# Layer-2 cross-attention: the self-attention's units regrouped across the four row groups of the array

## The reference

```
q, k = rope(x @ Wq), rope(x @ Wk)                    # 128 tokens, 32 heads of 8
w    = softmax(max(q k^T / sqrt(8) + mask, lowest))  # 128 x 128 per head
a_w  = tanh(gate) * softmax(q a_k^T / sqrt(8))       # 128 x 2048 per head: a_k = context @ Wk
out  = (w @ v + a_w @ a_v) @ Wo
```

## Time and profile before

| | |
|---|---|
| three runs | 1271.54, 1272.19, 1277.94 us |
| profiled execution, first to last instruction | 1179.2 us |
| what lies around the span, against the median | 93.0 us |
| PE busy in the span | 1060.2 us (90%) |
| DVE busy | 684.4 us (58%) |
| ACT busy | 486.5 us (41%) |
| main loop of L2X | from 429.8 to 736.5 us of the span |

### The profile page before, as it was taken

The page is one execution under the profiler, slowest core; times in us unless marked ns, Lnnn a source line. Parts: engine busy times, 40 slices in busy tenths (PEclk is TensorE's granted clock), DMA queues, the critical chain, the costliest instruction groups (busy, mean ns, idle before and its releaser), DMA issues.

```text
span 1179.2 us, 23059 instructions
## 1 busy us (share of the span) xinstructions
PE 1060.2 (90%) x9433; PEld 747.2 (63%) x9433; DVE 684.4 (58%) x1528; ACT 486.5 (41%) x1097; POOL 167.7 (14%) x172
## 2 busy tenths in 40 slices
PE   7988899996995999999999999898999990887998
PEld 6866666664884555555555665677566660776776
DVE  4544257775326667765556752454768997555333
ACT  2111137773331335556456568352544540141332
POOL 0002300000000000000000000000777776100000
PEclk9999999997997999999999999899999995988999
DMA  9113300000301200000000000201556554005661
GB/s 357 57 41 121 126 1 2 2 3 29 146 1 51 121 1 1 2 2 2 1 2 2 2 2 2 87 1 62 141 148 187 151 146 123 16 1 223 224 223 54
DMA packets 16727, 84.39 MB, mean 72 GB/s; under 512 B 3184, under 2 KB 4208, under 8 KB 12912
## 3 DMA queue, kind: packets, MB, share of 16 engines
q1 hardware_dynamic: 8432, 57.75, 12.9%
q0 software_dynamic: 8192, 25.17, 7.5%
HBM read 82.65 MB, written 0.26 MB: 70 GB/s over the span
## 4 chain that ended last, share of the span: by engine, by line
PE 71%; DVE 15%; POOL 7%; issue 4%; ACT 2%; DMA 1%; POOLq 0%; SPq 0%; DVEq 0%; ACTq 0%
PE L2X_bank_ring L1799 7%; PE L2X_bank_ring L1815 7%; PE L2X_bank_read L1829 6%; POOL L2F_rows L2532 5%; PE L2X_bank_ring L1738 4%; DVE x L2768 3%; PE L1X_banks_scores L927 3%; PE L2X_bank_ring L1747 3%; PE L3F_bank_y L3409 3%; PE L1A_bank_qk L1192 2%; PE L0X_bank_moments L473 2%; PE L0X_bank_k L462 2%; PE L3F_bank_gate_up L3369 2%; PE L1X_bank_proj L904 2%; PE L1X_bank_read L943 2%
## 5 line engine op out<-in xcount | busy, mean ns | idle before, releaser
L2098 DVE TENSOR_REDUCE L2X_max_parts<-L2X_bank_ring 128x1 f32<-128x512 f32 x256 | 158.3, 683 | 85.9 <-PE L2X_bank_ring L1799 85.9
L2009 ACT ACTIVATE L2X_context_exp<-L2X_bank_ring 128x384 f32<-128x384 f32 (+1 forms) x384 | 144.1, 464 | 63.0 <-PE L2X_bank_ring L1815 60.3
L2532 POOL DMA_INDIRECT L2F_rows<-in_L2F_embed_dram,L2F_expert x128 | 131.7, 1029 | 56.2 <-issue 37.3
L1799 PE MATMUL L2X_bank_ring<-L2X_context_kT,L2X_q_masked 32*128 32x512 f32 x512 | 97.4, 630 | 0.0
L1035 ACT ACTIVATE L1X_probs<-L1X_clipped,L1X_drop,L1X_keep 128x1024 f32<-128x1024 f32 x64 | 77.6, 1237 | 30.7 <-DVE L1X_clipped L1095 23.5
L1095 DVE TENSOR_SCALAR L1X_clipped<-L1X_banks_scores 128x1024 f32<-128x1024 f32 x64 | 75.4, 1220 | 24.6 <-PE L1X_banks_scores L927 22.9
L1815 PE MATMUL L2X_bank_ring<-L2X_q_and_max,L2X_context_kT 32*128 32x384 f32 (+1 forms) x768 | 85.9, 497 | 0.0
L1829 PEld LDWEIGHTS L2X_bank_read<-L2X_context_exp,L2X_context_v_ones 128*32 128x32 f32 x2048 | 50.2, 109 | 43.8 <-issue 33.4
L1829 PE MATMUL L2X_bank_read<-L2X_context_exp,L2X_context_v_ones 128*32 128x128 f32 x2048 | 75.8, 277 | 1.1 <-ACT L2X_context_exp L2009 0.8
L2768 DVE SCALAR_TENSOR_TENSOR x<-L2F_rows,L2F_expert_weight,x 128x256 f32<-128x256 f32 x128 | 62.4, 487 | 4.6
L1799 PEld LDWEIGHTS L2X_bank_ring<-L2X_context_kT,L2X_q_masked 32*128 32x128 f32 x512 | 41.4, 183 | 24.7 <-issue 12.2
(11 more groups left out here) (632 smaller groups left out, 2027.5 us busy)
## 6 DMA issues: line engine op xcount, KB each, us to landing
L3F_expert_weights<-in_L3F_experts_dram SPq DMA_DIRECT2D x16, 1280.0 KB, 5.7
L1A_groups<-in_L1A_groups_dram SPq DMA_DIRECT2D x3, 1536.0 KB, 9.7
L0X_tokens<-in_L0X_tokens_dram SPq DMA_DIRECT2D x8, 512.0 KB, 13.3
ctxT<-in_ctxT_dram SPq DMA_DIRECT2D x7, 512.0 KB, 13.9
slot<-in_L1A_dram SPq DMA_DIRECT2D x1, 3584.0 KB, 11.6
slot<-in_L0F_dram SPq DMA_DIRECT2D x1, 3072.0 KB, 10.9
slot<-in_L2A_dram SPq DMA_DIRECT2D x1, 3072.0 KB, 10.5
slot<-in_L2F_dram SPq DMA_DIRECT2D x1, 2476.5 KB, 9.1
```

Of the source, the lines that this page charges most:

```text
L1799: nc.tensor.matmul(bank[:, :], qm[32 * g:32 * g + 32, b, c, j, :], cT[32 * g:32 * g + 32, s % 3, blk * 512:(blk + 1) * 512], start=True, s ...
L2009: nc.scalar.activation(ex[:, n % NE, g, 0:width(s)], bank_of(s_e, done(n) + g + 1)[:, 0:width(s)], ACT.Exp, scale=SCALE).then_inc(s_e, 1)
L2098: nc.vector.tensor_reduce(parts[:, j, g, blk:blk + 1], bank_of(s_ft, n)[:, :], AX, ALU.max).then_inc(s_ft, 1)
L2532: pool.indirect_dma_start(out=rows[:, r, k, :], out_offset=None, in_=env.dram["L2F_embed"], in_offset=bass.IndirectOffsetOnAxis(idx[:, b, ...
```

## The change: what it does

The 64 heads of the small attention are cut into 16 units instead of 24. A unit is now (s, j): head j of each of the four row groups, so always four heads, and a stage has as many units as a group has heads: three or two. Unit (s, x) takes the places of the old unit of quarter x; quarter 3 of every stage, and quarter 2 too in stages 0 and 5, has none. `self_scores` writes its four products each into a bank of its own in the ring (four places instead of one), and `self_shift` empties them with four instructions of 128 columns; its row maximum, subtraction, the exponential, the four transposes and their copy are 512 columns wide. `self_read` writes to four column groups, `turn_reads` transposes `heads(c)` slices of soT instead of four. The mask is loaded once per batch instead of three times side by side.

```diff
-EXTRA_L2X = {"L2X_mask": lambda i: np.repeat(i["mask_Bx1xSxS_fk0"].reshape(B, 1, P, P), 3, 1).transpose(2, 0, 1, 3).reshape(P, B * 3 * P)}
+EXTRA_L2X = {"L2X_mask": lambda i: i["mask_Bx1xSxS_fk0"].reshape(B, P, P).transpose(1, 0, 2).reshape(P, B * P)}
...
-    maskt = L.sb("mask", [P, B * TRIO])
+    maskt = L.sb("mask", [P, B * P])
...
-    smx = L.sb("self_max", [P, 3])
-    se, spT = L.sb("self_exp", [P, TRIO]), L.sb("self_probsT", [P, TRIO])
-    soT = L.sb("self_readT", [P, NG, P])
+    smx = L.sb("self_max", [P, NG])
+    se, spT = L.sb("self_exp", [P, NG * P]), L.sb("self_probsT", [P, NG * P])
+    soT = L.sb("self_readT", [P, 3, P])
...
-    def heads_read(n):
-
-        return sum(heads(stages[m // NG][1]) for m in range(n))
+    units = [(s, j) for s in range(NSTG) for j in range(heads(stages[s][1]))]
+    NU = len(units)
+
+    def unit(s, x):
+
+        s, x = s + x // 4, x % 4
+        return units.index((s, x)) if (s, x) in units else None
...
         def self_scores(n):
-            (b, c), g = stages[n // NG], n % NG
-            bank = turns.take(pe, s_st, n + 1)
-            for j in range(heads(c)):
-                i = nc.tensor.matmul(bank[:, j * P:(j + 1) * P], qm[32 * g:32 * g + 32, b, c, j, :],
-                                     kT[32 * g:32 * g + 32, c, b, :], start=True, stop=True)
-            i.then_inc(s_ss, 1)
+            (s, j) = units[n]
+            b, c = stages[s]
+            for g in range(NG):
+                bank = turns.take(pe, s_st, NG * n + g + 1)
+                nc.tensor.matmul(bank[:, 0:P], qm[32 * g:32 * g + 32, b, c, j, :],
+                                 kT[32 * g:32 * g + 32, c, b, :], start=True, stop=True).then_inc(s_ss, 1)
 
         def self_turn(n):
             pe.wait_ge(s_se, n + 1)
             bank = turns.take(pe, s_spT, n + 1)
-            for j in range(heads(stages[n // NG][1])):
-                i = nc.tensor.transpose(bank[:, j * P:(j + 1) * P], se[:, j * P:(j + 1) * P], ident)
+            for g in range(NG):
+                i = nc.tensor.transpose(bank[:, g * P:(g + 1) * P], se[:, g * P:(g + 1) * P], ident)
             i.then_inc(s_sturn, 1)
...
         def self_read(n):
-            (b, c), g = stages[n // NG], n % NG
+            (s, j) = units[n]
+            b, c = stages[s]
             pe.wait_ge(s_spT, n + 1)
             bank = turns.take(pe, s_soc, n + 1)
-            for j in range(heads(c)):
+            for g in range(NG):
                 h = head_at(c, g, j)
-                nc.tensor.matmul(bank[32 * j:32 * j + 32, 0:P], svp[:, b, h * VW:h * VW + 32],
-                                 spT[:, j * P:(j + 1) * P], start=True, stop=True).then_inc(s_so, 1)
+                nc.tensor.matmul(bank[32 * g:32 * g + 32, 0:P], svp[:, b, h * VW:h * VW + 32],
+                                 spT[:, g * P:(g + 1) * P], start=True, stop=True).then_inc(s_so, 1)
 
         def turn_reads(s):
-            pe.wait_ge(s_soc, NG * (s + 1))
+            pe.wait_ge(s_soc, units_before(s + 1))
             bank = turns.take(pe, s_sy, s + 1)
-            for g in range(NG):
-                i = nc.tensor.transpose(bank[:, g * P:(g + 1) * P], soT[:, g, :], ident)
+            for j in range(heads(stages[s][1])):
+                i = nc.tensor.transpose(bank[:, j * P:(j + 1) * P], soT[:, j, :], ident)
             i.then_inc(s_sot, 1)
...
-                n, r = NG * s + t // 4, t % 4
+                x, r = t // 4, t % 4
+                n, following, past = unit(s, x), unit(s, x + 1), unit(*(s, x - 1) if x else (s - 1, 3))
                 firsts = first_sets(s, t)
                 second_scores(s, t)
                 if v_tile(s, t):
                     context_v(*v_tile(s, t))
                 if firsts:
                     first_scores(*firsts[0])
-                if r == 3 and n + 1 < NG * NSTG:
-                    self_scores(n + 1)
+                if r == 3 and following is not None:
+                    self_scores(following)
...
-                if r == 0 and n:
-                    self_read(n - 1)
+                if r == 0 and past is not None:
+                    self_read(past)
                 if r == 1 and s + 2 < NSTG:
                     context_k(s + 2, t // 4)
-                if r == 2:
+                if r == 2 and n is not None:
                     self_turn(n)
...
         read(NSTG - 1, NT - 1)
-        self_read(NG * NSTG - 1)
         turn_reads(NSTG - 1)
...
         def self_exp(n):
             act.wait_ge(s_sd, n + 1)
-            wd = width(n // NG)
-            nc.scalar.activation(se[:, 0:wd], se[:, 0:wd], ACT.Exp).then_inc(s_se, 1)
+            nc.scalar.activation(se[:, :], se[:, :], ACT.Exp).then_inc(s_se, 1)
 
         def self_copy(n):
             act.wait_ge(s_sturn, n + 1)
             if n:
-                act.wait_ge(s_so, heads_read(n))
-            wd = width(n // NG)
-            nc.scalar.activation(spT[:, 0:wd], bank_of(s_spT, n + 1)[:, 0:wd], ACT.Copy).then_inc(s_spT, 1)
+                act.wait_ge(s_so, NG * n)
+            nc.scalar.activation(spT[:, :], bank_of(s_spT, n + 1)[:, :], ACT.Copy).then_inc(s_spT, 1)
 
         def self_copy_read(n):
-            s, g = n // NG, n % NG
-            wd = 32 * heads(stages[s][1])
-            act.wait_ge(s_so, heads_read(n + 1))
-            if s and g == 0:
+            s, j = units[n]
+            act.wait_ge(s_so, NG * (n + 1))
+            if s and j == 0:
                 act.wait_ge(s_sot, s)
-            nc.scalar.activation(soT[0:wd, g, :], bank_of(s_soc, n + 1)[0:wd, 0:P], ACT.Copy).then_inc(s_soc, 1)
+            nc.scalar.activation(soT[:, j, :], bank_of(s_soc, n + 1)[:, 0:P], ACT.Copy).then_inc(s_soc, 1)
...
-                if r == 0 and m:
-                    self_copy_read(m - 1)
+                if r == 0 and past is not None:
+                    self_copy_read(past)
+                if r == 1 and m is not None:
+                    self_exp(m)
                 if r == 1:
-                    self_exp(m)
                     if s + 2 < NSTG:
                         context_k(s + 2, t // 4)
-                if r == 2:
+                if r == 2 and m is not None:
                     self_copy(m)
         copy_read(NSTG - 1)
-        self_copy_read(NG * NSTG - 1)
         tail.scalar(act)
 
...
         def self_shift(n):
-            (b, c) = stages[n // NG]
-            wd, nh = width(n // NG), heads(c)
-            dve.wait_ge(s_ss, n + 1)
+            b = stages[units[n][0]][0]
             if n:
                 dve.wait_ge(s_sturn, n)
-            nc.vector.scalar_tensor_tensor(out=se[:, 0:wd], in0=bank_of(s_st, n + 1)[:, 0:wd], scalar=SCALE,
-                                           in1=maskt[:, b * TRIO:b * TRIO + wd], op0=ALU.mult, op1=ALU.add).then_inc(s_st, 1)
-            dve.wait_ge(s_st, n + 1)
-            e = se[:, 0:wd].rearrange("p (j k) -> p j k", j=nh)
-            chain(nc.vector.tensor_reduce(smx[:, 0:nh], e, AX, ALU.max))
-            chain(nc.vector.tensor_scalar(smx[:, 0:nh], smx[:, 0:nh], LOWEST, None, ALU.max))
-            nc.vector.scalar_tensor_tensor(out=e, in0=e, scalar=LOWEST, in1=smx[:, 0:nh].unsqueeze(2).to_broadcast([P, nh, P]),
+            for g in range(NG):
+                dve.wait_ge(s_ss, NG * n + g + 1)
+                nc.vector.scalar_tensor_tensor(out=se[:, g * P:(g + 1) * P], in0=bank_of(s_st, NG * n + g + 1)[:, 0:P], scalar=SCALE,
+                                               in1=maskt[:, b * P:(b + 1) * P], op0=ALU.mult, op1=ALU.add).then_inc(s_st, 1)
+            dve.wait_ge(s_st, NG * (n + 1))
+            e = se[:, :].rearrange("p (g k) -> p g k", g=NG)
+            chain(nc.vector.tensor_reduce(smx[:, :], e, AX, ALU.max))
+            chain(nc.vector.tensor_scalar(smx[:, :], smx[:, :], LOWEST, None, ALU.max))
+            nc.vector.scalar_tensor_tensor(out=e, in0=e, scalar=LOWEST, in1=smx[:, :].unsqueeze(2).to_broadcast([P, NG, P]),
                                            op0=ALU.max, op1=ALU.subtract).then_inc(s_sd, 1)
...
-            o = bank_of(s_sy, s + 1)[:, :].rearrange("p (g j e) -> p g j e", g=NG, e=32)[:, :, 0:nh, :]
+            o = bank_of(s_sy, s + 1)[:, 0:width(s)].rearrange("p (j g e) -> p g j e", g=NG, e=32)
...
-                if t % 4 == 3 and n + 1 < NG * NSTG:
-                    self_shift(n + 1)
+                if t % 4 == 3 and following is not None:
+                    self_shift(following)
...
```

More of the change, by code:

```diff
@@ L1669, in done, with units_before @@
         return NG * n
-    def heads_read(n):
-        return sum(heads(stages[m // NG][1]) for m in range(n))
+    units = [(s, j) for s in range(NSTG) for j in range(heads(stages[s][1]))]
[3 more added lines that the diff above has]
+        return units.index((s, x)) if (s, x) in units else None
+    def units_before(s):
+        return sum(u < s for u, _ in units)
     sets = [4 * heads(c) for _, c in stages]
@@ L2003, in _ @@
             for t in range(NT):
```

(9 more changed lines are left out.)

## The result

| | kernel before | changed kernel |
|---|---|---|
| median of 13 runs each | 1272.37 us (1263.07 to 1277.94) | 1278.08 us (1273.33 to 1284.09) |
| ratio to before | | 1.0047, 95% interval 1.0025 to 1.0070 |
| L2X, residual sum to residual sum | 361.4 us | 368.65 us |
| its main loop, first to last second score | 302.8 us | 310.8 us |

The changed kernel is slower by 0.47% (5.7 us; interval 3.2 to 8.9). Forecast were 1278.9 us and +6.7 us.

The account below looks back on a forecast made before the run. PE's order of work was taken as the path, held at places by the seven-bank ring. Terms -8.7 + 2.2 - 0.9 + 14.4 + 1.0 - 0.4 - 0.9 = +6.7 us gave 1278.9 us, range 1268 to 1285.

Parts of the forecast that it names:

- thirteen places with first scores: Next tile's last second score waits for self_shift: eight places cost 0.93 us each, five cost 1.40, together +14.4 us.
- the loop's start: Fourteenth place with first scores: tile 0's last second score and tile 1's places come later, +1.0 us.
- parts 1 and 2: Eight missing units save 8.7 us of PE's path; the remaining wider ones cost 2.2; turn_reads saves 0.9.
- two places without first scores: t = 15 of stage 4, t = 3 of stage 5: DVE takes banks at once, four parallel groups save, -0.4 us.
- the end: Layer's end: last unit read eight tiles earlier, DVE's first two divide steps done earlier, L2080 starts sooner, -0.9 us.
- 0.9 us waits for the shift: Sign of being right: PE waits for L2056 before a second score, 0.9 us in stages 1, 3, 4, thirteen places in all.
- waits for DVE near 14 us: Sign of being wrong: PE's waits for DVE, 13.8 us in all before, stay near 14 us.
- The other signs: Stage 3: four tiles with a unit grow about 1 us, without one shrink 1.3; DVE's idle time vanishing means wrong.
- the 93 us around the span: Profiled span 1179.2 us leaves 93.0 us to the runs' median 1272.19; the change touches nothing of them.
- A: Rival at the thirteen places: the ring does not hold PE, so faster, -13.4 us, 1258.8 us; chance 0.12.
- B: Rival: PE's present ring waits absorb half of the 15.4 us delay, -1.0 us, 1271.2 us; chance 0.20.
- C: Rival: DVE's longer chain bounds the three-head stages, 9 us on top, 1288 us; chance 0.10.

Follow-up runs that it names:

- experiment 1: Changed kernel with the first-score maxima at t % 4 == 3 reading 256 of 512 columns: loop 301.6 us against 310.8, ratio 0.9967 to the kernel before.
- 2: Kernel before with the first-score maxima at t % 4 == 3 reading 256 of 512 columns: loop 302.6 us against 302.8, ratio 1.0014.
- experiment 4: Changed kernel with self_shift's 512-column row maximum done twice: loop 311.2 us against 310.8, ratio 1.0065 to the kernel before.
- fifth experiment: Kernel before, unchanged, profiled again: span 1271.1 us, gather 230 us, loop 302.8 us, end 10.84 us.
- 9: Two-bank units of 6, PE issuing the first bank's products before the second's in stages 1, 3, 4, 5 and at loop's start: loop 303.1 us, ratio 0.9979.
- 10: Changed kernel with two-bank units, PE waiting for the second bank only after issuing the first bank's products: loop 300.5 us, ratio 0.9955 to the kernel before.
- 3: Changed kernel with a unit's self scores and self_shift moved from t % 4 == 3 to t % 4 == 0, scores behind self_read: loop 303.0 us, ratio 0.9987.
- 6: Changed kernel with each four-head unit in two banks (three heads and one, or two and two) instead of four: loop 303.0 us, ratio 0.9979.
- 7: Two-bank units of 6 with scores and shift moved to t % 4 == 0 behind self_read: loop 304.7 us, ratio 0.9986.
- 8: Kernel before with three and six idle products (results unread) in PE's gaps at the layer's end: end 9.58 us instead of 10.84, ratio 0.9966.
- 11: Kernel of 10 with the idle products of 8: loop 300.4 us, end 9.15 us, ratio 0.9958 to the kernel before.

## Why the prediction was right, step by step

Loop and edges of the layer, from the two traces: ahead of the loop +1.42 us, loop +8.02, end -2.18, together +7.26 against +6.7 forecast. The whole time grew by 5.7 us, with 7.26 inside its interval (3.2 to 8.9).

| step | forecast | measured |
|---|---|---|
| thirteen places with first scores | +14.4 | +14.4 (stages 1, 3, 4: 0.74 to 1.02; stages 0, 2: 1.35 to 1.40) |
| the loop's start | +1.0 | +1.0 (+1.42 ahead of the loop, -0.46 in its first two tiles) |
| parts 1 and 2: fewer units, wider ones, `turn_reads` | -7.4 | -7.2 (what is left of the loop) |
| two places without first scores | -0.4 | +1.25 |
| the end | -0.9 | -2.2 |

The places are read as the growth of tile t % 4 == 3 and the next one, with the absent `self_read` (0.21 us) added back at t = 15. The mechanism is shown by the weight loads 0.05 us behind the first shift at all thirteen places, and by experiments 1, 2 and 4. The third row is what remains, but single tiles bear it out: in stages 1 to 4, tile 11 fell by 0.67 us (0.67 forecast for the scores), tile 14 by 0.31 to 0.33 (0.38 for the turn), and tile 6 grew by 0.11 (one more transpose).

**Luck in the sum.** Two terms were mis-sized, by +1.65 and -1.3 us, and nearly cancel; the total is closer than its terms. At the places two smaller errors cancel. I had read the 0.05 us between a release and PE's start from a weight load, and the last group's first matmul starts 0.28 us behind the release (0.18 at the first place), 1.17 us late at the place above and not 0.94; but its second matmul follows after 0.20 us instead of 0.43, and so the group ends up 0.94 late after all.

**Right in size, in part at another place: the loop's start.** I had the delay in tiles 0 and 1. Most of it lies ahead of the loop, where the fourth self score waits for DVE's first maximum:

```profile
431.80 0.48 PE L1770 MATMUL L2X_bank_ring<-L2X_self_kT,L2X_q_masked 32*128 32x128 f32 x2 [0.55 <-DVE L2X_max_parts L2105]
```

Measured from the sum into x ahead of the layer, the maxima of tile 1 start 0.74 us later than in the kernel before, where I had 1.0.

**Mis-sized, the places without first scores.** The step said that DVE takes the banks at once. It does, but I had asked only who frees S1 for the next tile, and not what S1 to S4 themselves wait for. With four places, S4 waits at t = 15 of stage 4 for the first exponential of its own tile, and at t = 3 of stage 5 S3 and S4 wait for `divide` and an exponential. The chain of the changed kernel goes there from PE to ACT and back (start us, us on the chain):

```profile
717.08 0.94 PE L2X_bank_ring L1824 x8
718.02 0.50 ACT L2X_context_exp L2016
718.51 0.04 issue
718.56 0.48 PE L2X_bank_ring L1770 x2
```

Tile 15 of stage 4 grew by 0.68 us, tile 3 of stage 5 by 0.57. The same waits spread the scores at the thirteen places (+0.33 us to the tile in stage 3 where I had them end as before), but there they are absorbed, since the last second score waits for DVE anyway.

**Mis-sized, the end.** DVE is done 0.8 us sooner, as computed (0.9). The other 1.4 us are the clock, of which the forecast said nothing. In the three profiles of the kernel before (the first, the fifth experiment's, and the second's with its shorter maxima) the granted clock stands at 0.50, the lower level of 1.2 GHz, for 3.4 us of the last matmuls; in the changed kernel it stays at 1.00 up to the layer's end. From the first:

```profile
738.10:741.50 3.40, 3.40 (x14) 3.12 (x14) 0.00 (x0) 0.60 (x1) 0.00 (x0) 0.50 0.00 0
```

The 1.4 us are not a sure gain of the change: experiments 9 and 10, whose ends have the same gaps as the changed kernel's, lost it. The changed kernel also has such a stretch of 3.4 us in the next part, from 756.4 us on, and that part, to the following sum into x, takes 62.3 us against 61.9.

**Wrong, what would show it.** I expected 0.9 us waits for the shift in the list of waits. That view shows none; the duration of the second scores does. I had also named waits for DVE near 14 us as a sign of being wrong, and they are 17.0: by the view of waits alone the forecast would have looked nearly refuted. The other signs held: in stage 3 the four tiles from a place with a unit on (3 to 6, 7 to 10) grew by 1.1 us, and those from tile 11 on, without one, shrank by 1.0 (1.3 forecast), and DVE's idle time did not vanish (its wait for first scores grew from 79.1 to 91.2 us). And the 93 us around the span were the difference between two executions, most likely on two chips, and not launch and end. The forecast survives, because it added a difference to the median.

**The rivals.** A falls: the last group starts behind the shift at all thirteen places. Its price was too high as well: with the wait taken away in experiment 1 the scores stay spread, and the layer is 2.0 us shorter than before, not 13.4. B falls: the places cost their full 14.4 us, so the other waits at the ring took up nothing. C falls by experiment 4.

## What to carry to other kernels

When work is spread over more banks, walk the ring from each use to the use that frees its place, in both directions: what the new uses wait for, and what now waits for them. A wait of one instruction in four hides in the duration of its group; look at how long a parallel group takes, not only at idle time. And of several banks, take each one right before its first product.

## What the runs showed of the hardware

**The clock behind short gaps.** At the layer's end PE stands idle in short gaps: 0.77, 0.53 and 1.40 us in the kernel before, 0.20, 0.49, 0.21 and 1.18 us in the changed one. Behind them the granted clock fell from 1.00 to 0.50 for 3.4 us in the kernel before (three profiles, ends 10.8 us) and in experiments 9 and 10 (10.05 and 9.9 us). Within the layer it did not fall in the changed kernel and experiments 1, 3, 4, 6 and 7 (8.7 us), whose gaps are those of experiments 9 and 10. With idle products in the gaps it stayed at 1.00 up to the layer's end in experiments 8 and 11; in the eleventh it fell 5 us behind it. What decides it in the kernels with like gaps stays open.

**A freed bank.** At the thirteen places the weight load started 0.05 us after the instruction that freed the bank had ended, and the matmul 0.28 us after it (0.18 at the first place).

**The gather.** The same 128 indirect transfers took 154 to 157 us on some chips and 223 to 230 on others (fifth experiment).
